# Wide attention: values held as weights, softmax sums from a block of ones, and a reordered load block

## The chip, the cores and the metric

The kernel runs on one core of a Trainium2 chip. The metric is the device time of one execution in microseconds (us). Before the change three executions took 2512.74 us in the median (2504.58 to 2514.27).

## What is computed

x is 16 sequences of 256 rows of 128 floats. Eight layers follow one another, each x = x + layer(layernorm(x)); the kernel has them in six blocks: wide attention, experts with slope attention, experts with rope attention, group attention, a recurrent layer, group attention. Only the first and the loads ahead of it are changed:

```python
def _L0_attn_a_ref(x, Wq, Wk, Wv, Wo, bo):          # N_HEADS = 16, HEAD_DIM = 64, DIM = 128
    q = (x @ Wq).reshape(b, s, N_HEADS, HEAD_DIM)    # likewise k and v
    dot = jnp.einsum('bihd,bkhd->bhik', q, k)
    w = jax.nn.softmax(dot / jnp.sqrt(jnp.float32(HEAD_DIM)), axis=-1)
    a = jnp.einsum('bhij,bjhd->bihd', w, v)
    return a.reshape(b, s, N_HEADS * HEAD_DIM) @ Wo + bo
...
x = x + _L0_attn_a_ref(_layernorm(x, axis=-1), L0_attn_a_Wq, L0_attn_a_Wk, L0_attn_a_Wv, L0_attn_a_Wo, L0_attn_a_bo)
```

## The kernel before, in words

x stays in SBUF for the whole kernel (`K.X`, 32 tiles of 128 rows, two a sequence). The program is a row of blocks; at the end of each all engines meet.

**Load block** (`load`, L95 to L185). SyncE's queue issues four transfers of x (L115) and then every weight of every layer in the order in which the program lists them (L117), the wide layer's five (`w_q`, `w_k`, `w_v`, `w_o`, `b_o`) last, then one small transfer `rows_dram` (L119), and waits for all (L120, L121). Meanwhile GpSimd (POOL) builds constants, and VectorE (DVE) takes the statistics of the 32 tiles once all of x is there (L184).

**Wide block** (`wide_attention`, L1905 to L2174). It begins with the layer norm's factors (`norm_stats`, L188, used by every layer), while POOL fills the ones' column of `va`, `parts` and the table `pick` (L2160 to L2168); the table takes a fill and six selects over 128x2048 elements. VectorE waits for those (L2134), scales `w_q` (L2136), and only then may TensorE start (L2036).

The work of sequence n + 1 (stage A), n (stage B) and n - 1 (stage E) is interleaved by `wide_schedule` (L1880) in nine slots; every engine walks the same list:
- A: `norm` turns the normalized rows (L1966), `qk` makes q and k of a pair of heads (L1972, copied by ScalarE at L2054, cast to bf16 by POOL at L2157), `max` makes bf16 scores (L1983) whose row maxima VectorE takes (L2098), `v` makes the values (L1976, copied by VectorE at L2089), `split` and `turnmax` bring the maxima into rows (L2101 to L2110).
- B: `score` makes the scores turned, keys on the partitions: two bf16 matmuls with `pick` put the negated maximum into the bank (L1999) and four f32 matmuls add k.q (L2003); ScalarE takes the exponential (L2059). `value` (L2014) multiplies: the probabilities are the stationary operand (128x128, four loads a head), and the values with a column of ones are the moving one (65 columns). So the sum stands beside the 64 outputs, queries on the partitions. `divide` is a reciprocal of 128x4 (L2116) and a product (L2118).
- E: `attn` turns the result by 16 transposes (L2023), copied by VectorE (L2093), and `project` multiplies by `w_o` (L2032), VectorE adds it to x (L2124) and takes the statistics (L2129).

Two PSUM banks hold the maxima (`Sb`), two the scores (`Tb`), two the values' output (`Ob`), and two are shared by all other pieces (`Mb`, with the semaphores `full` and `drained`). An f32 matmul and its weight load appear as two records each in the trace, an f32 transpose and a bf16 matmul as one. In `scores` and `maxima` the two heads of a pair lie on partitions 0 to 63 and 64 to 127 and use the two row halves of the array.

Elsewhere, in the group layer's `value` (L724), the values are already the stationary operand: four heads of 32 columns each write to four partition ranges of one bank.

## Time and profile before

| | |
|---|---|
| median of three executions | 2512.74 us |
| profiled execution, its own time | 2513.31 us |
| its span, first to last instruction | 2511.3 us |
| load block | 0 to 40.3 us |
| wide block | 40.3 to 788.3 us |
| busy in the whole span: TensorE, VectorE, ScalarE, POOL | 86%, 57%, 46%, 24% |

All durations below are from the profiled execution. PE is TensorE, PEld its weight loads, DVE VectorE, ACT ScalarE, POOL GpSimd, SPq the DMA issues of SyncE. In a timeline a row gives the start and the time up to the end of what it merges; the start of the next row of the same engine says when the array could go on, since the ends overlap the next piece.

### The profile page before, as it was taken

What the parts mean: (1) busy time and instruction counts of PE and PEld (TensorE: products, weight loads), DVE (VectorE), ACT (ScalarE), POOL (GpSimd) and SP (SyncE); (2) the same over time, 40 slices, a digit from 0 to 9 for tenths busy, and PEclk for the clock granted to TensorE, in tenths of its full rate; (3) what the DMA queues carried; (4) which work ended last, traced back from release to release, by engine and by line L of the source; (5) the groups of instructions that cost most, each with busy time, mean ns of one, the idle gap of its engine ahead of it and who ended that gap; (6) DMA issues with size and microseconds to landing.
All of it is one profiled execution on the core that took longest, in us unless ns stands there. A gap on an engine that the chain in (4) does not pass through costs nothing. (4 is left out here: it accounts for less than half of the span.)

```text
span 2511.3 us, 53791 instructions
## 1 busy us (share of the span) xinstructions
PE 2157.5 (86%) x21439; PEld 1560.5 (62%) x21439; DVE 1429.7 (57%) x2854; ACT 1158.7 (46%) x1979; POOL 602.0 (24%) x952
## 2 busy tenths in 40 slices
PE   0899999999998799788868998999669997469996
PEld 0687877877787689655547896666435543234543
DVE  1545454454542443466644445776568885768883
ACT  0333333333324233366553323665647775537774
POOL 4111111111100322133203232443123331433330
PEclk9999999999997899899978998999869998669998
DMA  5000000000000002245400022444134440034441
GB/s 156 1 1 1 1 1 1 1 1 1 1 1 1 6 5 51 51 108 117 95 2 4 1 52 53 109 116 93 25 84 107 110 105 2 2 92 108 107 106 49
DMA packets 142790, 121.04 MB, mean 48 GB/s; under 512 B 11808, under 2 KB 127408, under 8 KB 142548
## 3 DMA queue, kind: packets, MB, share of 16 engines
q1 hardware_dynamic: 142548, 117.64, 19.7%
q8 instruction: 172, 2.82, 0.5%
q14 instruction: 70, 0.57, 0.1%
HBM read 63.48 MB, written 54.12 MB: 47 GB/s over the span
## 5 line engine op out<-in xcount | busy, mean ns | idle before, releaser
L890 DVE TENSOR_REDUCE l_group_mx<-maxima 128x4 f32<-128x1024 f32 x248 | 303.9, 1226 | 77.1 <-PE maxima L683 75.6
L2059 ACT ACTIVATE l_wide_pr<-scores 128x512 f32<-128x512 f32 x256 | 139.0, 594 | 408.7 <-PE scores L2003 408.7
L818 ACT ACTIVATE l_group_pr<-scores 128x1024 f32<-128x1024 f32 x256 | 261.7, 1022 | 72.2 <-PE scores L704 70.0
L2014 PEld LDWEIGHTS bank<-l_wide_va,l_wide_pr 128*128 128x128 f32 x2048 | 254.2, 192 | 36.0 <-issue 33.2
L2014 PE MATMUL bank<-l_wide_va,l_wide_pr 128*128 128x65 f32 x2048 | 254.5, 271 | 0.0
L2098 DVE TENSOR_REDUCE l_wide_mx<-maxima 128x2 f32<-128x512 f32 x256 | 165.1, 687 | 92.2 <-PE maxima L1983 92.2
L2157 POOL CAST l_wide_qk<-l_wide_qk 128x512 bf16<-128x512 f32 x128 | 78.7, 615 | 390.6 <-ACT l_wide_qk L2054 390.6
L890 DVE TENSOR_REDUCE l_slope_mx<-maxima 128x6 f32<-128x768 f32 x124 | 118.9, 959 | 78.2 <-PE maxima L690 76.8
L890 DVE TENSOR_REDUCE l_rope_mx<-maxima 128x6 f32<-128x768 f32 x124 | 118.8, 958 | 58.8 <-PE maxima L690 57.9
L818 ACT ACTIVATE l_slope_pr<-scores 128x768 f32<-128x768 f32 x128 | 103.6, 810 | 91.0 <-PE scores L711 90.8
L724 PE MATMUL bank<-l_group_pr,va 128*32 128x256 f32 x2048 | 145.3, 403 | 0.0
L683 PE MATMUL maxima<-l_group_st 50*128 50x256 bf16 x992 | 102.4, 286 | 45.7 <-DMA l_group_st<-mask_dram 16.9
L818 ACT ACTIVATE l_rope_pr<-scores 128x768 f32<-128x768 f32 x128 | 103.8, 811 | 77.4 <-PE scores L711 77.2
L2003 PE MATMUL scores<-l_wide_qk 64*128 64x256 f32 x1024 | 132.3, 378 | 0.0
L2093 DVE COPY l_wide_att_t<-bank 128x512 f32<-128x512 f32 x64 | 44.3, 692 | 140.8 <-PE bank L2023 140.8
L704 PE MATMUL scores<-l_group_st 53*128 53x256 bf16 x1024 | 103.3, 281 | 16.4 <-ACT l_group_pr L818 11.8
L2054 ACT ACTIVATE l_wide_qk<-bank 128x512 f32<-128x512 f32 x128 | 76.4, 597 | 72.6 <-PE bank L1972 72.6
L2003 PEld LDWEIGHTS scores<-l_wide_qk 64*128 64x128 f32 x1024 | 99.2, 190 | 10.0
L683 PEld LDWEIGHTS maxima<-l_group_st 50*128 50x128 bf16 x992 | 35.2, 97 | 89.0 <-DVE l_group_mx L890 40.3
L1972 PE MATMUL bank<-l_wide_xnt,w_q 128*128 128x256 f32 x256 | 88.1, 426 | 0.5 <-ACT l_wide_xnt L2051 0.5
L1613 ACT ACTIVATE l_rope_e_ht<-maxima 128x512 f32<-128x512 f32 x64 | 38.1, 595 | 108.5 <-PE maxima L1562 108.4
L1613 ACT ACTIVATE l_slope_e_ht<-maxima 128x512 f32<-128x512 f32 x64 | 38.1, 595 | 107.3 <-PE maxima L1562 107.2
(456 smaller groups left out, 4721.5 us busy)
## 6 DMA issues: line engine op xcount, KB each, us to landing
l_group_st<-stack_dram SPq DMA_DIRECT2D x64, 384.0 KB, 6.0
l_slope_st<-stack_dram SPq DMA_DIRECT2D x32, 384.0 KB, 5.6
l_rope_st<-stack_dram SPq DMA_DIRECT2D x32, 384.0 KB, 5.6
stack_dram<-l_group_parts SPq DMA_DIRECT2D x64, 192.0 KB, 2.3
stack_dram<-l_group_parts SPq DMA_DIRECT2D x64, 128.0 KB, 1.9
stack_dram<-l_slope_parts SPq DMA_DIRECT2D x32, 192.0 KB, 2.4
stack_dram<-l_rope_parts SPq DMA_DIRECT2D x32, 192.0 KB, 2.3
stack_dram<-l_slope_parts SPq DMA_DIRECT2D x32, 128.0 KB, 2.3
```

What stands on the lines that cost most here:

```text
L683: ins = pe.matmul(Mx[:, z, first:first + keys], st[at, b % KEEP, 0, i, t * P:(t + 1) * P], st[at, b % KEEP, 1, i, 0:keys], start=(t == 0 o ...
L704: ins = pe.matmul(Tp[:, z, t * S:t * S + S - first], st[at, b % KEEP, 1, i, t * P:(t + 1) * P], st[at, b % KEEP, 0, i, first:S], start=(t ...
L724: ins = pe.matmul(Ob[i // 2][32 * z:32 * z + 32, (i % 2) * S + first:(i % 2) * S + S], va[:, b % KEEP, t, h // G, :], pr[:, (h // 2) % AHE ...
L818: act.activation(pr[:, i % AHEAD, :, 0:keys], Tp[:, :, 0:keys], ACT.Exp).then_inc(s["exps"], 1)
L890: dve.tensor_reduce(mx[:, b % 2, :, :, i], max_bank(i, b)[:, :, 0:BLOCKS * keys].rearrange("p z (a k) -> p z a k", k=keys), AX.X, ALU.max, ...
L1972: ins = pe.matmul(bank[:, z * S:(z + 1) * S], w[:, i * P:(i + 1) * P], xnt[:, nxt, :], start=True, stop=True)
L2003: ins = pe.matmul(Tb[z][:, t * S:(t + 1) * S], qk[rows(z), par, i, 1, t * P:(t + 1) * P], qk[rows(z), par, i, 0, :], start=False, stop=(t ...
L2014: ins = pe.matmul(Ob[i // 2 % 2][:, col:col + D64 + 1], pr[:, i % WIDE_AHEAD, kt * S + t * P:kt * S + (t + 1) * P], va[:, par, kt, i, :], ...
L2054: act.activation(qk[:, nxt, i].rearrange("p z s -> p (z s)"), Mb[b][:], ACT.Copy).then_inc(drained[b], 1)
L2059: act.activation(pr[:, h % WIDE_AHEAD, :], Tb[h % 2][:], ACT.Exp).then_inc(s["exps"], 1)
L2098: dve.tensor_reduce(mx[:, nxt, :, h], Sb[h % 2][:].rearrange("p (t k) -> p t k", k=S), AX.X, ALU.max, negate=True).then_inc(s["maxed"], 1)
L2157: pool.tensor_copy(qk16[:, nxt, i], qk[:, nxt, i]).then_inc(s["half"], 1)
```

## The change

Load block: SyncE issues x, then `w_q` and `w_k` (waited for in the block), then `w_v`, `w_o`, `b_o` (with a semaphore of their own, waited for in the wide block), then `rows_dram`. The 22 other transfers move to SyncE of the wide block. Each quarter of x has its own semaphore, and VectorE starts on a quarter when it has come. `pick` is made in this block: POOL builds a 128x16 table, and ScalarE spreads it to 128x16x128; `parts` and a 128x64 block of ones are filled here too.

Wide block: the list of pieces is one walk over all sequences (`wide_slots`, `wide_walk`), eight slots a sequence. In `value` the stationary operand is a head's 128x64 values and the moving one the probabilities (128x256); head z of a pair writes partitions 64z to 64z + 63. POOL adds the two key tiles of the probabilities (two additions of 128x256 a pair), and in `sum` a 128x64 block of ones as weights gives the sums, repeated on 64 partitions. `divide` becomes a reciprocal of 128x256 and a product of 128x256, which writes `att_t` directly: `attn`, its transposes and copies go. ScalarE copies the values instead of VectorE. `project` is split into two pieces.

```diff
-def load(nc, K, loads):
+def load(nc, K, first, behind, behind_s):
...
-                sp.dma_start(K.X[:, tiles, :], K.x_in[:, tiles, :]).then_inc(x_loaded, 16)
-            for dst, src in loads:
+                sp.dma_start(K.X[:, tiles, :], K.x_in[:, tiles, :]).then_inc(x_loaded[n], 16)
+            for dst, src in first:
                 sp.dma_start(dst, src).then_inc(loaded, 16)
+            for dst, src in behind:
+                sp.dma_start(dst, src).then_inc(behind_s, 16)
             sp.wait_ge(rows_copied, 1)
             sp.dma_start(K.rows_dram, row_rows[:]).then_inc(rows_kept, 16)
-            sp.wait_ge(loaded, 16 * len(loads))
+            sp.wait_ge(loaded, 16 * len(first))
...
+            act.wait_ge(eye_built, 1)
+            act.activation(K.pick[:], heads_eye[:].unsqueeze(2).to_broadcast([P, H, P]), ACT.Copy).then_inc(picked, 1)
...
+            c.done(pool.memset(heads_eye[:], 0.0))
+            for z in range(2):
+                for j in range(3):
+                    select(heads_eye[:], ALU.not_equal, 1.0, -(64 * z + H * j), [[-1, H]], 1)
+            pool.sem_inc(eye_built, 1)
+            c.done(pool.memset(K.ones[:], 1.0))
+            c.done(pool.memset(K.parts[:], 0.0))
...
+                if t % (TILES // parts) == 0:
+                    dve.wait_ge(x_loaded[t // (TILES // parts)], 16)
...
+def wide_slots():
+    slots = []
+    for i in range(PAIRS):
+        slot = [("divide", (i - 2) % PAIRS, -1 if i < 2 else 0), ("score", i, 0)]
+        slot += [("turnmax", 0, 1)] if i == 7 else []
+        slot += [("max", (i + 1) % PAIRS, 2 if i + 1 >= PAIRS else 1)]
+        slot += [("split", 0, 1)] if i == 6 else []
+        slot += [("qk", (i + 2) % PAIRS, 2 if i + 2 >= PAIRS else 1)]
+        slot += [(what, (i - 1) % PAIRS, -1 if i < 1 else 0) for what in ("value", "sum")]
+        slot += {1: [("v", 0, 1)], 2: [("v", 1, 1)], 3: [("v", 2, 1), ("xn", 0, 2)], 4: [("project", 0, -1)],
+                 5: [("v", 3, 1), ("norm", 0, 2)], 6: [("project", 1, -1)]}.get(i, [])
+        slots += slot
+    return slots
...
+        def max_banks(i, b):
+            return Tb if b == 0 and i % 2 else Sb
...
+        @block.sync
+        def _(sp):
+            for dst, src in late:
+                sp.dma_start(dst, src).then_inc(late_s, 16)
+            sp.wait_ge(behind_s, 16 * 3)
+            sp.wait_ge(late_s, 16 * len(late))
...
-                        if i % 2 == 0:
-                            wait(pe, s["divided"], o_t.add() - 2)
-                        pe.wait_ge(s["exps"], exps_t.add())
-                        for t in range(NT):
-                            col = ((i % 2) * NT + t) * (D64 + 1)
-                            for kt in range(NT):
-                                ins = pe.matmul(Ob[i // 2 % 2][:, col:col + D64 + 1],
-                                                pr[:, i % WIDE_AHEAD, kt * S + t * P:kt * S + (t + 1) * P], va[:, par, kt, i, :],
-                                                start=(kt == 0), stop=(kt == NT - 1))
-                        ins.then_inc(s["valued"], 1)
...
+                    wait(pe, s["divided"], p - 1)
+                    pe.wait_ge(s["exps"], 2 * p + 2)
+                    for kt in range(NT):
+                        for z in range(2):
+                            ins = pe.matmul(Ob[i % 2][rows(z), 0:S], va[:, at, kt, 2 * i + z, :],
+                                            pr[:, i % 2, z, kt * S:(kt + 1) * S], start=(kt == 0), stop=(kt == NT - 1))
+                    ins.then_inc(s["valued"], 1)
+                elif what == "sum":
+                    pe.wait_ge(s["added"], 2 * p + 2)
+                    for z in range(2):
+                        ins = pe.matmul(Ob[i % 2][rows(z), S:2 * S], ones[:], tiles_sum[:, i % 2, z, :], start=True, stop=True)
+                    ins.then_inc(s["summed"], 1)
+                elif what == "project":
+                    pe.wait_ge(s["divided"], PAIRS * (b + 1))
+                    for c in range(PAIRS):
+                        ins = pe.matmul(bank[:, 0:C], att_t[:, at, c, i * P:(i + 1) * P], W["wo"][:, c, :],
+                                        start=(c == 0), stop=(c == PAIRS - 1))
...
+                elif what == "v":
+                    act.wait_ge(full[m], count)
+                    act.activation(va[:, at, i // 2, 8 * (i % 2):8 * (i % 2) + 8, :].rearrange("p h d -> p (h d)"),
+                                   Mb[m][:], ACT.Copy).then_inc(drained[m], 1)
+                elif what == "score":
+                    wait(act, s["valued"], p - 1)
+                    wait(act, s["added"], 2 * (p - 1))
+                    for z in range(2):
+                        act.wait_ge(s["scored"], 2 * p + z + 1)
+                        act.activation(pr[:, i % 2, z, :], Tb[z][:], ACT.Exp).then_inc(s["exps"], 1)
...
-            dve.wait_ge(s["pool_set"], POOL_SETS)
...
+                elif what == "divide":
+                    dve.wait_ge(s["summed"], p + 1)
+                    wait(dve, s["divided"], p)
+                    own.done(dve.reciprocal(rc[:], Ob[i % 2][:, S:2 * S]))
+                    dve.tensor_tensor(att_t[:, at, i, :], Ob[i % 2][:, 0:S], rc[:], ALU.mult).then_inc(s["divided"], 1)
...
+                elif what == "score":
+                    wait(pool, s["summed"], p - 1)
+                    for z in range(2):
+                        pool.wait_ge(s["exps"], 2 * p + z + 1)
+                        pool.tensor_tensor(tiles_sum[:, i % 2, z, :], pr[:, i % 2, z, 0:S], pr[:, i % 2, z, S:2 * S],
+                                           ALU.add).then_inc(s["added"], 1)
...
+        late, first, behind = loads[:-5], loads[-5:-3], loads[-3:]
...
-                wide_attention(nc, K, name, W_wide)
+                wide_attention(nc, K, name, W_wide, late, behind_s, late_s)
```

In the new list POOL casts `qk` after the two additions of the slot, VectorE takes `divide` of the pair before last ahead of the slot's maxima, and TensorE's order in a slot is score, (turnmax), max, qk, value, sum, and then v, norm or half of project where the slot has one.

## Rows read from the trace of the kernel before

**Rows 1.** Windows, 400 to 500 us: PE, PEld, DVE, ACT, POOL busy; clock, DMA.

```profile
400.00:500.00 100.00, 98.39 (x751) 80.03 (x750) 49.90 (x107) 33.15 (x63) 13.75 (x22) 1.00 0.00 1
```

**Rows 2.** Timeline of PE: start, us, line, tiles, count, idle before.

```profile
402.10 0.61 PE L2023 MATMUL bank<-ident,l_wide_att 128*128 128x128 f32 x4
402.54 1.00 PE L2014 MATMUL bank<-l_wide_va,l_wide_pr 128*128 128x65 f32 x8
403.48 0.39 PE L1999 MATMUL scores<-l_wide_shift,l_wide_pick 64*128 64x512 bf16 x2
...
404.57 0.38 PE L1983 MATMUL maxima<-l_wide_qk 64*128 64x256 bf16 x4
404.88 0.70 PE L1972 MATMUL bank<-l_wide_xnt,w_q 128*128 128x256 f32 x2
...
405.85 1.00 PE L2014 MATMUL bank<-l_wide_va,l_wide_pr 128*128 128x65 f32 x8
...
426.75 3.84 PE L2032 MATMUL bank<-w_o,l_wide_att_t 128*128 128x128 f32 x32
...
434.15 0.39 PE L1999 MATMUL scores<-l_wide_shift,l_wide_pick 64*128 64x512 bf16 x2
...
436.58 0.39 PE L1999 MATMUL scores<-l_wide_shift,l_wide_pick 64*128 64x512 bf16 x2 [0.81 <-ACT l_wide_pr L2059]
...
745.86 0.39 PE L1999 MATMUL scores<-l_wide_shift,l_wide_pick 64*128 64x512 bf16 x2
...
773.40 3.68 PE L2014 MATMUL bank<-l_wide_va,l_wide_pr 128*128 128x65 f32 x32
```

**Rows 3.** Timeline of all engines, load block and start of the wide block.

```profile
10.51 6.29 DVE L184 BATCH_NORM_STATS2 moments<-x 128x6 f32<-128x128 f32 x32 [10.51 <-DMA x<-in_L_attn_a_x_dram]
...
33.31 0.53 SPq L119 DMA_DIRECT2D rows_dram<-row_rows  x1
...
42.84 12.77 POOL L2168 TENSOR_SCALAR_AFFINE_SELECT l_wide_pick<-l_wide_pick 128x2048 bf16<-128x2048 bf16 x6
...
56.91 0.69 PE L1966 MATMUL bank<-ident,l_wide_xn 128*128 128x128 f32 x2 [51.79 <-DVE w_q L2136]
```

**Rows 4.** Transfers, 0 to 100 us: GB/s in 40 slices of 2.5 us.

```profile
GB/s 32 282 290 292 229 108 61 356 406 326 289 287 150 390 346 55 3 3 0 0 0 0 0 0 0 0 0 0 0 0 0 0 7 0 0 0 0 0 0 0
```

**Rows 5.** Timeline of DVE, the same norm factors at the slope block's start.

```profile
788.37 0.21 DVE L196 TENSOR_TENSOR mean<-moments 128x32 f32<-128x32 f32 x1 [1.10 <-PEq L1908]
...
790.28 0.19 DVE L213 SCALAR_TENSOR_TENSOR shift<-mean,rstd 128x32 f32<-128x32 f32 x1
```

**Rows 6.** Timeline, first sequence's q, k and maxima, up to its first score.

```profile
68.60 0.60 ACT L2054 ACTIVATE l_wide_qk<-bank 128x512 f32<-128x512 f32 x1 [1.25 <-PE bank L1972]
...
69.37 0.62 POOL L2157 CAST l_wide_qk<-l_wide_qk 128x512 bf16<-128x512 f32 x1 [1.23 <-ACT l_wide_qk L2054]
...
77.04 0.39 PE L1983 MATMUL maxima<-l_wide_qk 64*128 64x256 bf16 x4 [0.40 <-DVE l_wide_mx L2098]
...
80.49 0.39 PE L1999 MATMUL scores<-l_wide_shift,l_wide_pick 64*128 64x512 bf16 x2 [0.39 <-DVE l_wide_shift L2110]
```

**Rows 7.** Timeline of PE, group layer: values as weights in four column ranges.

```profile
2033.01 1.07 PE L724 MATMUL bank<-l_group_pr,va 128*32 128x256 f32 x16
2034.02 0.39 PE L704 MATMUL scores<-l_group_st 53*128 53x256 bf16 x4
```

**Rows 8.** Groups by line and shape: busy us, mean ns, idle before.

```profile
L2116 DVE RECIPROCAL l_wide_rc<-bank 128x4 f32<-128x4 f32 x128 | 23.2, 181 | 69.7 <-PE bank L2014 63.2
L211 DVE RECIPROCAL rstd<-rstd 128x32 f32<-128x32 f32 x8 | 2.8, 353 | 2.6 <-ACT rstd L217 2.4
...
L2118 DVE TENSOR_TENSOR l_wide_att<-bank,l_wide_rc 128x256 f32<-128x256 f32 x128 | 54.3, 424 | 4.4
L2098 DVE TENSOR_REDUCE l_wide_mx<-maxima 128x2 f32<-128x512 f32 x256 | 165.1, 687 | 92.2 <-PE maxima L1983 92.2
L2153 POOL TENSOR_TENSOR x<-x,b_o 128x256 f32<-128x256 f32 x16 | 11.6, 725 | 190.4 <-ACT l_wide_xn L2066 190.4
```

More of the change, by code:

```diff
@@ L99, in load @@
         loaded = nc.alloc_semaphore(name="loaded")
-        x_loaded = nc.alloc_semaphore(name="x_loaded")
+        x_loaded = [nc.alloc_semaphore(name=f"x_loaded{n}") for n in range(4)]
         own = nc.alloc_semaphore(name="pool_own")
@@ L1874 @@
 D64 = 64
-WIDE_BANK = {"norm": (0,), "qk": (1, 0, 1, 0, 1, 0, 1, 0), "attn": (1, 0, 1, 0), "v": (1, 0, 1, 0), "project": (1,),
-             "turnmax": (0,)}
-WIDE_AHEAD = 4
-def wide_schedule(do_a, do_b, do_e):
-    early_a = {0: [("norm", 0)], 1: [("qk", 0), ("qk", 1)], 2: [("qk", 2), ("qk", 3)], 3: [("max", 0), ("qk", 4)],
-               4: [("max", 2), ("qk", 6)], 5: [("max", 4), ("v", 1)], 6: [("max", 6), ("v", 3)], 7: [("split", 0)],
-               8: [("turnmax", 0)]}
-    late_a = {3: [("max", 1), ("qk", 5)], 4: [("max", 3), ("qk", 7), ("v", 0)], 5: [("max", 5), ("v", 2)], 6: [("max", 7)]}
-    early_e = {1: [("attn", 0)], 2: [("attn", 2)], 7: [("project", 0)]}
-    late_e = {1: [("attn", 1)], 2: [("attn", 3)]}
-    pieces = []
-    for slot in range(PAIRS + 1):
-        if do_b and slot < PAIRS:
-            pieces.append(("score", slot))
-        for a, e, head in ((early_a, early_e, 0), (late_a, late_e, 1)):
-            if do_a:
-                pieces += a.get(slot, [])
-            if do_e:
-                pieces += e.get(slot, [])
-            if do_b and slot > 0:
-                pieces.append(("value", 2 * slot - 2 + head))
-        if do_b and slot > 0:
-            pieces.append(("divide", slot - 1))
-    return pieces
@@ L1905, in wide_attention @@
-def wide_attention(nc, K, name, W):
-    fills = [sum(b == m for banks in WIDE_BANK.values() for b in banks) for m in range(2)]
+def wide_slots():
[11 more added lines that the diff above has]
+    return slots
@@ new lines, in wide_walk @@
+def wide_walk():
+    slots, order, counts = wide_slots(), [], [0, 0]
+    bank = {}
+    for what, i, _ in slots:
+        if what in ("norm", "qk", "v", "project", "turnmax"):
+            bank[what, i] = len(bank) % 2
+    for n in range(-2, NB + 1):
+        for what, i, ahead in slots:
+            if 0 <= n + ahead < NB:
+                m = bank.get((what, i))
+                if m is not None:
+                    counts[m] += 1
+                order.append((what, i, n + ahead, m, counts[m] if m is not None else None))
+    return order
@@ L1933, in wide_attention @@
         block = ctx.enter_context(nc.Block(name))
-        POOL_SETS = 6
-        def rows(h):
-            return slice(64 * (h % 2), 64 * (h % 2) + 64)
-        def fill_tallies():
-            return [Tally(s["full0"], fills[0]), Tally(s["full1"], fills[1])]
-        def bank_of(tallies, what, i):
-            if what not in WIDE_BANK:
-                return None, None
-            b = WIDE_BANK[what][i]
-            return b, tallies[b].add()
+        order = wide_walk()
+        filling = {(what, i, b): (m, count) for what, i, b, m, count in order}
@@ L2140, in _ @@
+            dve.wait_ge(s["stats"], TILES)
         @block.gpsimd
         def _(pool):
[L2142 to L2157 removed]
@@ L2173, in _ @@
-            ins.then_inc(set_, 3)
-            batches(pool, tallies, step)
+            for what, i, b, m, count in order:
+                at, p = b % 2, PAIRS * b + i
+                if what == "norm":
+                    pool.wait_ge(s["xn"], b + 1)
+                    if b == 0:
+                        pool.wait_ge(behind_s, 16 * 3)
+                    x = K.X[:, b * NT:(b + 1) * NT, :]
+                    pool.tensor_tensor(x, x, W["bias"].unsqueeze(1).to_broadcast([P, NT, C]), ALU.add).then_inc(s["biased"], 1)
+                elif what == "qk":
+                    pool.wait_ge(drained[m], count)
+                    pool.sem_inc(s["waited"], 1)
+                    pool.tensor_copy(qk16[:, at, i], qk[:, at, i]).then_inc(s["half"], 1)
+                elif what == "score":
+                    wait(pool, s["summed"], p - 1)
+                    for z in range(2):
+                        pool.wait_ge(s["exps"], 2 * p + z + 1)
+                        pool.tensor_tensor(tiles_sum[:, i % 2, z, :], pr[:, i % 2, z, 0:S], pr[:, i % 2, z, S:2 * S],
+                                           ALU.add).then_inc(s["added"], 1)
@@ L2273, in program @@
         W_wide = {"wq": w_q[:], "wk": w_k[:], "wv": w_v[:], "wo": w_o, "bias": b_o[:]}
-        load(nc, K, loads)
+        K.ones, K.parts, K.pick = sb("ones", [P, D64]), sb("parts", [P, 2, NT, 2, 64], BF16), sb("pick", [P, H, P], BF16)
+        late, first, behind = loads[:-5], loads[-5:-3], loads[-3:]
+        for_wide.enter_context(nc.cleanup_on_exit())
+        behind_s, late_s = nc.alloc_semaphore(name="behind"), nc.alloc_semaphore(name="late")
+        load(nc, K, first, behind, behind_s)
         for n, layer in enumerate(LAYERS):
```

308 lines of the change are left out of this document (110 added, 198 removed).

## The prediction, made before the changed kernel had run

> **What bounds the kernel now.** I read the windows first. In the middle of the wide block TensorE is busy for 98.39 of 100 us at full clock, VectorE for 49.9, ScalarE for 33.2, POOL for 13.8 [rows 1]. So there the time is TensorE's list of pieces, and an edit on another engine counts only if TensorE waits for it. Next the timeline of PE, with the cost of a piece taken as the distance to the next start [rows 2]. The first score of one sequence starts at 434.15, that of the sequence seven later at 745.86: 44.53 us a sequence. A score piece costs 403.48 to 404.57 = 1.09, a max piece 0.31, a qk piece 0.97, a value piece of one head 402.54 to 403.48 = 0.94 (four in a row take 3.68, so 0.92; I use 0.93), a transpose piece 0.44, project up to 3.8 for both halves. At the start of each sequence TensorE waits 0.81 us for the exponentials of slot 0.
>
> The value pieces, 16 x 0.93 = 14.9 us, are a third of a sequence. A head is four f32 products of 65 columns. A qk piece streams two f32 products of 256 columns in 0.97 us, so by columns four of 65 would take about half of the 0.93: the weight loads of 128 columns set their pace.
>
> Last, the timeline of all engines up to TensorE's first real work [rows 3]. SyncE issues its last transfer at 33.31 us, the blocks change at 40.3, POOL then builds `pick` from 42.84 to 55.61, and TensorE starts at 56.91 with [51.79 <-DVE w_q]: VectorE's scaling of `w_q` stands behind POOL's table. Nothing but loading and preparation happens for 57 us.
>
> **The load block.** It ends when `rows_dram` has landed. After the change it stands behind x and the wide layer's five transfers only, 4160 KB instead of 9.8 MB (the slices together). The first four slices move 2.24 MB in 10 us [rows 4], and x is complete at 10.51 [rows 3]. The 2.1 MB left, at the 290 to 400 GB/s of the full slices, take 5.3 to 7.2 us, then `rows_dram` and the change of block about 1.5: 17 to 19, I take 18. Other work in this block is earlier: POOL's list grows by eight small operations and a fill, and ScalarE's spread of 2048 elements a partition, by 0.60 us for 512 [rows 6], is at most 2.4 us. Gain **22.3 us**. The 22 transfers that move to SyncE of the wide block have that queue to themselves, nobody there waits for them, and the wide block is far longer than their 30 us; POOL's queue issues none.
>
> **Start of the wide block.** The norm factors take 788.37 to 790.47 = 2.1 us where no POOL work runs beside [rows 5], and `w_q` 1.3 more (55.61 to 56.91 with the wait [rows 3]). So TensorE starts 3.5 us into the block, not 16.6: gain **13.1 us**.
>
> **First sequence.** Before, TensorE's start to its first score was 56.91 to 80.49 = 23.6 us [rows 3, 6], with four qk pieces made ahead. The new walk has max(i + 1) and then qk(i + 2), so each pair waits for its own chain: qk 0.97, to ScalarE 0.2, copy 0.60, to POOL 0.17 (68.60 + 0.60 to 69.37), cast 0.62, to TensorE 0.1, max 0.31 = 2.97 us [rows 2, 6]. Norm and the first qk and cast take about 4.5 us, seven steps 20.8, split and turnmax 3.5 less the wait already in 77.04 to 80.49 [rows 6], and qk of the next sequence stands before the score, 1.3: in all 29.8. Loss **6.2 us**. If TensorE stays at half clock (it did in its first pieces), up to 7 x 1.3 = 9 more.
>
> **A sequence in steady state.** Value and sum of a pair become six f32 products of 256 columns in two column halves. The wide trace has no 64-column weights. Nearest is the group layer: eight such products in four column ranges take 2033.01 to 2034.02 = 1.01 us [rows 7], where one after another at half a qk piece (0.43 to 0.49) they would take over 3.4. So ranges run side by side. With two ranges six products are three rounds of 0.43 = 1.28, plus the 0.15 that the 1.01 has over two rounds, plus 0.11 for a weight load that nothing covers: 1.55 us a pair, where 2 x 0.93 = 1.86 stood. Bounds: 1.3 if all loads hide, 2.85 if halves don't overlap. I take 1.55, since rows 7 is the same product with only the width changed. Sequence: 44.53 - 14.9 - 4 x 0.44 - 0.8 (score 0 now has max, qk, value and sum behind it) + 8 x 1.55 + 0.1 (project in two) = **39.5 us**.
>
> The Trainium skill, TensorEngine Tiling, Key Properties, says that a change of tiling mode drains the array, and the new slot goes row halves, full, column halves, row halves. If each of 128 value groups paid a drain of 0.17 us, what 402.10 + 0.61 overlaps its successor by, instead of my 0.11, the sum would be 8 us higher; no row here shows a change from full to column halves.
>
> **What covers the rest.** VectorE: copies of values and `att_t` leave it, and the reciprocal grows from 4 to 256 elements a partition. It takes 0.181 us for 4 and 0.353 for 32 [rows 8], so 6.1 ns an element and 1.72 us. A slot is 1.72 + 0.42 (product) + 2 x 0.69 (maxima) + 0.1 = 3.6 us against TensorE's 1.09 + 0.31 + 0.97 + 1.55 = 3.92; the slots with split or project are longer on TensorE too. Hidden, with 0.3 us to spare in the barest slot. The divide is needed only two slots later. POOL: two additions of at most 0.73 each (the row has a repeated operand, a lower bound; 1.0 is my upper) and a cast: 2.1 to 2.6 of 3.92. The cast ends near 4.1 after the slot's start, and its max starts at 3.92 + 1.09 = 5.0: hidden, 0.9 to spare. ScalarE adds four copies of 0.6 a sequence to a third of its time: hidden. If one of these covers goes, the stall is in TensorE's order before max or value.
>
> **Sum.** After the first score: first sequence (no value of a former one, no project) 39.5 - 1.55 - 3.8 = 34.2; 13 x 39.5 = 513.5; the last but one without look-ahead (0.31 + 2 x 0.97 + 0.45) 36.8; the last, eight scores and groups 8 x 2.64 + 3.8 = 24.9; the end 1.55 + 0.5 (additions) + 2.3 (divide) + 3.7 (project) + 1.0 + 1.1 = 10.2. Together 619.6, against 80.49 to 788.3 = 707.8: gain **88.2 us**. Total 22.3 + 13.1 - 6.2 + 88.2 = 117.4 us. The profiled execution took 2513.3, half a microsecond over the median: **2396 us**. Other blocks don't change.
>
> **Rivals.**
> - *Load and start alone.* The groups cost what they replace, 2.2 us with the transposes, because loads of weights expose themselves in column halves too. Then 2513.3 - 22.3 - 13.1 + 6.2 = 2484. For it: value is paced by loads today. Against: rows 7, where 16 loads hide in 1.01 us. Chance 0.07.
> - *VectorE becomes the bound.* If the reciprocal from PSUM takes 3.0 rather than 1.72 us, a sequence on VectorE is 8 x (3.0 + 0.42 + 1.37 + 0.2) + 2.4 = 42.3 and TensorE waits for maxima: 2.8 x 15.5 = 43 more, 2440. It decides from 2.6 us on. For it: 256 elements are eight times the longest reciprocal seen. Against: the slope from 4 to 32. Chance 0.09.
> - *Slower.* The column halves don't run side by side: value and sum stream 6 x 0.43 and cost 2.85 a pair. 128 pairs x 1.3 = +166: 2562. It decides from 0.92 us a pair on, where the 117.4 are gone, that is at 2.47. For it: no 64-column weights in the trace, and `sum` adds a third to the columns. Against: rows 7. Chance 0.05.
>
> **Numbers.** The forecast has 0.79. Its range: 1.3 instead of 1.55 a pair is -32, so 2364, with little chance; a further 0.15 a pair for switches +19, a first sequence at half clock +9, uneven slots with short VectorE stalls of 1 us a sequence +15: 2439, which also reaches the second rival. Range 2368 to 2442. A difference under 0.5%, 12.6 us, can't be told from none: faster 0.94 (the first two rivals too), same 0.01, slower 0.05.
>
> **What would show it.** Start of wide block near 18 and first PE piece 3.5 later; a new L for value and sum with starts 1.5 to 1.6 us apart; first scores of consecutive sequences 39.5 apart; reciprocal near 1.72 us; PE over 97% busy there with no wait on VectorE. A reciprocal over 2.6 us or groups over 2.4 would make me wrong; so would PE idling before max behind POOL's cast.

## The result, and the profile after

The changed kernel took 2400.79 us in the median of four executions (2398.14 to 2402.08), the kernel before beside it 2509.22. The ratio is 0.9566, 95% interval [0.9542, 0.9590]: faster. The profiled execution took 2402.08 us with a span of 2400.2. Forecast were 2396 us and 2368 to 2442.

The windows of the steady state (us, then PE, PEld, DVE, ACT, POOL busy, clock, DMA) answer to [rows 1]:

```profile
400.00:500.00 100.00, 100.00 (x717) 61.72 (x717) 77.04 (x106) 41.51 (x77) 40.82 (x63) 1.00 0.00 1
```

TensorE has no gap left, its weight loads are busy for 62 instead of 80 of 100 us, and VectorE rose from 50 to 77. The timeline of PE over a bare slot, one with a piece v and one with half of project answers to [rows 2] and [rows 7]:

```profile
308.26 1.13 PE L1997 MATMUL bank<-w_v,l_wide_xnt 128*128 128x512 f32 x2
309.32 0.39 PE L2020 MATMUL scores<-l_wide_shift,pick 64*128 64x512 bf16 x2
...
313.23 2.05 PE L2046 MATMUL bank<-w_o,l_wide_att_t 128*128 128x128 f32 x16
315.21 0.39 PE L2020 MATMUL scores<-l_wide_shift,pick 64*128 64x512 bf16 x2
...
330.53 0.39 PE L2020 MATMUL scores<-l_wide_shift,pick 64*128 64x512 bf16 x2
330.75 1.03 PE L2024 MATMUL scores<-l_wide_qk 64*128 64x256 f32 x8
331.62 0.38 PE L2004 MATMUL maxima<-l_wide_qk 64*128 64x256 bf16 x4
331.93 0.70 PE L1991 MATMUL bank<-l_wide_xnt,w_q 128*128 128x256 f32 x2
...
332.99 1.08 PE L2035 MATMUL bank<-l_wide_pr,l_wide_va 128*64 128x256 f32 x8
333.90 0.60 PE L2041 MATMUL bank<-l_wide_tiles_sum,ones 128*64 128x256 f32 x4
334.44 0.39 PE L2020 MATMUL scores<-l_wide_shift,pick 64*128 64x512 bf16 x2
...
370.54 0.39 PE L2020 MATMUL scores<-l_wide_shift,pick 64*128 64x512 bf16 x2
```

Value costs 332.99 to 333.90 = 0.91 us and sum 0.54, together 1.45 a pair (forecast 1.55). The bare slot is 330.53 to 334.44 = 3.91 (forecast 3.92), but qk takes 1.06 where it took 0.97, v 1.06 and half of project 1.98. The next sequence starts at 370.54: 40.01 us a sequence, forecast 39.5, before 44.53.

The load block and start, timeline of all engines, answer to [rows 3, 5, 6]:

```profile
5.02 1.64 DVE L200 BATCH_NORM_STATS2 moments<-x 128x6 f32<-128x128 f32 x8 [5.02 <-DMA x<-in_L_attn_a_x_dram]
...
9.10 2.08 SPq L123 DMA_DIRECT2D rows_dram<-row_rows  x1
...
16.04 0.24 POOL L147 TENSOR_SCALAR_AFFINE_SELECT not_first<-not_first 64x80 bf16<-64x80 bf16 x1
...
17.41 0.21 DVE L212 TENSOR_TENSOR mean<-moments 128x32 f32<-128x32 f32 x1 [5.36 <-PEq L97]
...
20.56 0.66 PE L1985 MATMUL bank<-ident,l_wide_xn 128*128 128x128 f32 x2 [15.45 <-ACT l_wide_xn L2059]
...
25.23 0.61 PE L2004 MATMUL maxima<-l_wide_qk 64*128 64x256 bf16 x4 [1.47 <-POOL l_wide_qk L2129]
...
29.31 0.61 PE L2004 MATMUL scores<-l_wide_qk 64*128 64x256 bf16 x4 [1.47 <-POOL l_wide_qk L2129]
...
41.14 0.39 PE L2004 MATMUL maxima<-l_wide_qk 64*128 64x256 bf16 x4 [0.61 <-POOL l_wide_qk L2129]
...
44.06 0.39 PE L2004 MATMUL scores<-l_wide_qk 64*128 64x256 bf16 x4 [0.61 <-POOL l_wide_qk L2129]
```

The wide block starts at 17.4 (forecast 18) and TensorE 3.2 us later (3.5). Then the first sequence: its maxima wait for POOL's cast as forecast, at first 4.08 us apart (25.23 to 29.31), later 2.92 (41.14 to 44.06; forecast 2.97). The early ones run their pieces at half the pace (the w_q part of a qk piece takes 25.77 to 26.78 = 1.01 us, later 41.46 to 42.00 = 0.54), and this lasts to about 38 us. The clock column of the windows reads 1.00 there, so it doesn't show this; the pieces do. The first score comes at 54.67.

Groups by line and shape, for [rows 8]:

```profile
L2105 DVE RECIPROCAL l_wide_rc<-bank 128x256 f32<-128x256 f32 x128 | 224.4, 1753 | 56.7 <-PE bank L2041 55.7
L2106 DVE TENSOR_TENSOR l_wide_att_t<-bank,l_wide_rc 128x256 f32<-128x256 f32 x128 | 54.3, 425 | 4.4
L2134 POOL TENSOR_TENSOR l_wide_tiles_sum<-l_wide_pr 128x256 f32<-128x256 f32 x256 | 180.5, 726 | 359.5 <-ACT l_wide_pr L2077 359.5
```

The reciprocal takes 1.753 us (forecast 1.72), the addition 0.726 (at most 0.73 to 1.0).

**Where the 111 us of the two profiled spans are.** The block behind the wide one starts at 788.37 before and at 687.11 after: 101.3 us come from load and wide block. The rest of the span is 1722.9 before and 1713.1 after, though nothing in it was changed. Stretches of all runs of this study, read from the timelines:

| run | wide block starts | first PE | first score | a sequence | wide block ends | rest of the span | median, us |
|---|---|---|---|---|---|---|---|
| before | 40.3 | 56.9 | 80.5 | 44.53 | 788.4 | 1722.9 | 2505 to 2513 |
| after | 17.4 | 20.6 | 54.7 | 40.01 | 687.1 | 1713.1 | 2400.8 |
| after_again | 18.1 | 21.3 | 54.7 | 40.01 | 686.1 | 1713.3 | 2404.1 |
| load_only | 18.0 | 21.1 | 44.5 | 44.53 | 752.7 | 1718.9 | 2472.2 |
| loads_first | 40.5 | 43.6 | 79.4 | 40.01 | 710.7 | 1706.9 | 2421.1 |
| one_half | 17.4 | 20.6 | 54.7 | 50.32 | 845.2 | 1723.1 | 2565.8 |
| short_reciprocal | 17.4 | 20.5 | 53.9 | 40.01 | 681.9 | 1722.4 | 2403.1 |
| product_twice | 18.0 | 21.1 | 55.0 | 40.01 | 688.1 | 1724.4 | 2409.1 |
| no_sum | 17.4 | 20.6 | 54.1 | 36.56 | 634.8 | 1713.3 | 2351.5 |
| bf16_sums | 17.3 | 20.5 | 54.5 | 37.43 | 646.6 | 1712.1 | 2371.0 |
| together | 18.1 | 21.2 | 54.7 | 38.98 | 670.4 | 1716.1 | 2393.0 |
| early_qk | 17.4 | 20.5 | 43.9 | 40.01 | 673.6 | 1722.4 | 2397.8 |
| both | 18.0 | 21.2 | 44.0 | 38.98 | 656.6 | 1709.6 | 2372.4 |
| all_three | 17.4 | 20.5 | 43.4 | 36.40 | 616.5 | 1718.1 | 2337.9 |

A sequence repeats to 0.01 us. The load block ends at 17.3 to 18.1 with the same code, and the wide block of the changed kernel at 687.1 and 686.1: its last piece, project, took 6.53 us at a granted clock of 0.56 in the one execution and 5.44 at 0.69 in the other. The rest of the span scatters by 17 us, and this goes with the clock too: the four runs where the windows show 0.91 for it (loads_first, both, bf16_sums, no_sum) took 1706.9 to 1713.3 us, the ten at 0.90 took 1713.1 to 1724.4. What lowers the clock wasn't tested. So effects are read from the stretches up to the end of the wide block, 1 to 3 us being open at that end, and the medians say whether they arrive.

### The profile page after: what moved, and what is told of

Its sections match the earlier page's. It is cut to its first block and busy times, and to the rows that moved or that the text cites. A ratio compares the mean times of both kernels' runs of the same rounds, so it can differ in the third digit from the quotient of the medians.

```text
span 2400.2 us, 52498 instructions
## 1 busy us (share of the span) xinstructions
PE 2097.6 (87%) x20671; PEld 1388.0 (58%) x20671; DVE 1555.6 (65%) x2742; ACT 1197.1 (50%) x2044; POOL 762.4 (32%) x1208
## 3 DMA queue, kind: packets, MB, share of 16 engines
q1 hardware_dynamic: 142548, 117.64, 20.6%
## 5 line engine op out<-in xcount | busy, mean ns | idle before, releaser
L906 DVE TENSOR_REDUCE l_group_mx<-maxima 128x4 f32<-128x1024 f32 x248 | 304.0, 1226 | 72.3 <-PE maxima L699 70.6
L2134 POOL TENSOR_TENSOR l_wide_tiles_sum<-l_wide_pr 128x256 f32<-128x256 f32 x256 | 180.5, 726 | 359.5 <-ACT l_wide_pr L2077 359.5
L2105 DVE RECIPROCAL l_wide_rc<-bank 128x256 f32<-128x256 f32 x128 | 224.4, 1753 | 56.7 <-PE bank L2041 55.7
L2089 DVE TENSOR_REDUCE l_wide_mx<-maxima 128x2 f32<-128x512 f32 x248 | 159.4, 685 | 32.5 <-PE maxima L2004 32.5
L2035 PE MATMUL bank<-l_wide_pr,l_wide_va 128*64 128x256 f32 x1024 | 138.8, 392 | 0.3 <-DVE l_wide_att_t L2106 0.3
L1001 POOL CAST l_group_cols<-l_group_mx 128x32 bf16<-128x32 f32 x32 | 6.7, 209 | 317.1 <-DVE l_group_mx L906 317.1
L2035 PEld LDWEIGHTS bank<-l_wide_pr,l_wide_va 128*64 128x64 f32 x1024 | 62.1, 136 | 61.0 <-issue 36.1
L2070 ACT ACTIVATE l_wide_va<-bank 128x512 f32<-128x512 f32 x64 | 38.2, 597 | 116.1 <-PE bank L1997 116.1
```

The source lines that it names most:

```text
L906: dve.tensor_reduce(mx[:, b % 2, :, :, i], max_bank(i, b)[:, :, 0:BLOCKS * keys].rearrange("p z (a k) -> p z a k", k=keys), AX.X, ALU.max, ...
L2035: ins = pe.matmul(Ob[i % 2][rows(z), 0:S], va[:, at, kt, 2 * i + z, :], pr[:, i % 2, z, kt * S:(kt + 1) * S], start=(kt == 0), stop=(kt == ...
L2089: dve.tensor_reduce(mx[:, at, :, 2 * i + z], max_banks(i, b)[z][:].rearrange("p (t k) -> p t k", k=S), AX.X, ALU.max, negate=True).then_in ...
L2105: own.done(dve.reciprocal(rc[:], Ob[i % 2][:, S:2 * S]))
L2134: pool.tensor_tensor(tiles_sum[:, i % 2, z, :], pr[:, i % 2, z, 0:S], pr[:, i % 2, z, S:2 * S], ALU.add).then_inc(s["added"], 1)
```

## The experiments

`load_only` is made from the kernel before, all others from the changed one.

**after_again**, the changed kernel itself. 

> The changed kernel once more, beside the kernel before on the same chip. Its wide block ended at 687 us against 788.3, a gain of 101 us, and everything behind it took 1713 against 1723 us though nothing there was changed. Theory (the 10 us behind the wide block are scatter between executions): the ratio is 0.957 to 0.960, and the blocks behind the wide one come within a few us of 1715 to 1723 again without a fixed sign. Rival (the change makes the later blocks faster, by its layout in SBUF or its loads): they take 1713 again and the kernel before 1723.

Measured: 2404.09 us, ratio 0.9599 [0.9581, 0.9618]. The rest took 1713.3 us again, which alone would fit the rival, but over all runs of the changed code it went from 1706.9 to 1724.4, both sides of the kernel before. The kernel before was profiled only once, but its medians of 2505.6 to 2509.2 lie 4 to 8 us under that profiled execution, so its 1722.9 is a long one. The 10 us are scatter; the change is worth what the end of the wide block shows, 101 to 102 us.

**load_only**, the old attention behind the new load block:

```diff
-        load(nc, K, loads)
+        load(nc, K, first, behind, behind_s)
...
+            for dst, src in late:
+                sp.dma_start(dst, src).then_inc(late_s, 16)
...
-        pick = sb("pick", [P, H, P], BF16)
+        parts, pick = K.parts, K.pick
```

> The kernel before with the new load block, pick and parts built there and the 22 late transfers in the wide block, and its old attention. Theory (load and start are worth 22.9 + 13.4 = 36 us and add to the rest): about 36 us under the kernel before, ratio 0.986, TensorE's first piece near 21 us, a sequence 44.5 us as before. Rival (the early start is lost again at once, because late transfers disturb the first sequence or the clock is lower): under 25 us.

Measured: 2472.18 us, ratio 0.9871 [0.9837, 0.9905], end of the wide block 788.4 to 752.7 = 35.7 us. The theory holds: the first score comes 36.0 us earlier, and nearly all of it is left at the end, so nothing is lost to the late transfers. It shows one thing more: TensorE's start to the first score takes 21.1 to 44.5 = 23.3 us with the old list and 20.6 to 54.7 = 34.1 with the new one. The new list costs 10.8 us here, not 6.2.

**loads_first**, the changed kernel with all transfers, and the waits for them, in the load block:

```diff
+            for dst, src in K.late:
+                sp.dma_start(dst, src).then_inc(K.late_s, 16)
             for dst, src in first:
                 sp.dma_start(dst, src).then_inc(loaded, 16)
...
+            sp.wait_ge(behind_s, 16 * 3)
+            sp.wait_ge(K.late_s, 16 * len(K.late))
```

> The changed kernel with all transfers in the load block again, in the old order. Theory (what ends the load block is the transfer issued last, and 5.6 MB of late weights stand ahead of it): the wide block starts near 40 instead of 17.4, the time is 23 us over the changed kernel, and TensorE starts 3.2 us into the block as in the changed kernel, since pick is not built there. Rival (POOL's longer list, which ended at 16.3, sets the block's end): under 5 us over it.

Measured: 2421.13 us, ratio 0.9670 [0.9649, 0.9692]; the wide block starts at 40.5, 23.1 us later, TensorE 3.2 us behind it, and the wide block ends 23.6 us later than after. The median is only 17 us over after_again; the rest of the span is the shortest of all here. Order of loads: 23 us of the 101.

**one_half**, no two column halves at once from the third pair on, the second head in columns of its own in the bank:

```diff
-                    for kt in range(NT):
-                        for z in range(2):
+                    for kt, z in [(kt, z) for kt in range(NT) for z in range(2)] if p < 2 else [(kt, z) for z in range(2) for kt in range(NT)]:
-                            ins = pe.matmul(Ob[i % 2][rows(z), 0:S], va[:, at, kt, 2 * i + z, :],
+                            ins = pe.matmul(Ob[i % 2][rows(z), 0:S] if p < 2 else Ob[i % 2][rows(0), z * S:(z + 1) * S],
+                                            va[:, at, kt, 2 * i + z, :],
...
-                        ins = pe.matmul(Ob[i % 2][rows(z), S:2 * S], ones[:],
+                        ins = pe.matmul(Ob[i % 2][rows(z), S:2 * S] if p < 2 else Ob[i % 2][rows(0), z * S:(z + 1) * S], ones[:],
```

> From the third pair on both heads' value and sum products write partitions 0 to 63, a head after the other, so that two column halves can't run at once; the sums and half of the outputs are then wrong values, the instructions are the same. Theory (the halves run side by side, value 0.91 us and sum 0.54): alone they stream 6 x 0.43 = 2.6 us, the slot grows by 1.2 us, 126 pairs, +140 to +160 us, which makes it slower than the kernel before by about 40. Rival (the group is limited by weight loads, not by columns): under +40 us.

Measured: 2565.77 us, ratio 1.0223 [1.0189, 1.0258], 50.32 us a sequence. Its timeline of PE:

```profile
331.82 1.94 PE L2034 MATMUL bank<-l_wide_pr,l_wide_va 128*64 128x256 f32 x8
333.60 1.03 PE L2040 MATMUL bank<-l_wide_tiles_sum,ones 128*64 128x256 f32 x4
334.56 1.12 PE L1997 MATMUL bank<-w_v,l_wide_xnt 128*128 128x512 f32 x2
```

The wide block ends 158 us later, inside the expected 140 to 160. The same products cost 1.78 and 0.96 instead of 0.91 and 0.54. The third rival's mechanism is real and has this price, +1.29 us a pair; the changed kernel is faster only because the halves do run side by side.

**short_reciprocal**, the divide's reciprocal over a quarter of the columns:

```diff
-                    own.done(dve.reciprocal(rc[:], Ob[i % 2][:, S:2 * S]))
-                    dve.tensor_tensor(att_t[:, at, i, :], Ob[i % 2][:, 0:S], rc[:], ALU.mult).then_inc(s["divided"], 1)
+                    own.done(dve.reciprocal(rc[:, 0:64], Ob[i % 2][:, S:S + 64]))
+                    dve.tensor_tensor(att_t[:, at, i, :].rearrange("p (a e) -> p a e", e=64), Ob[i % 2][:, 0:S].rearrange("p (a e) -> p a e", e=64),
+                                      rc[:, 0:64].unsqueeze(1).to_broadcast([P, 4, 64]), ALU.mult).then_inc(s["divided"], 1)
```

> The changed kernel with the reciprocal taken of 64 of the 256 queries and used four times over (wrong sums for three quarters), so that it costs some 0.55 us instead of 1.75. Theory (VectorE is hidden behind TensorE in every slot of the steady state): a sequence stays at 40.0 us, and only the end and the last sequence gain, 2 to 5 us in all. Rival (VectorE holds TensorE back somewhere): a sequence falls under 39 us, 15 us or more in all.

Measured: 2403.14 us, ratio 0.9571 [0.9526, 0.9616]; 40.01 us a sequence, unchanged to the hundredth, and the wide block ends 5.2 us earlier, 5.0 of it behind the last sequence's start, where project runs at full pace (3.81 us) too. VectorE isn't on the path in the steady state.

**product_twice**, VectorE loaded with a second product a pair:

```diff
+                    own.done(dve.tensor_tensor(att_t[:, at, i, :], Ob[i % 2][:, 0:S], rc[:], ALU.mult))
                     dve.tensor_tensor(att_t[:, at, i, :], Ob[i % 2][:, 0:S], rc[:], ALU.mult).then_inc(s["divided"], 1)
```

> The changed kernel with the product of the divide done twice, 0.47 us more on VectorE a pair, so 4.1 us in a bare slot against TensorE's 3.91. Theory (bare slots have 0.3 us to spare, and the work may slip into the slots with v and project since the divide is needed only two slots later): under 1 us a sequence, 0 to 15 us in all. Rival (VectorE is close to the bound and every addition shows): 0.47 x 128 = 60 us.

Measured: 2409.12 us, ratio 0.9596 [0.9551, 0.9641], against 2400.8 and 2404.1. Windows:

```profile
400.00:500.00 100.00, 100.00 (x716) 61.61 (x716) 83.09 (x127) 41.25 (x77) 41.17 (x63) 1.00 0.01 1
```

VectorE is busy for 83 instead of 77 us of 100, and a sequence takes 40.01 us still; the wide block ends 1 to 2 us later. But the run doesn't push VectorE over TensorE's slot, as was expected of it (4.1 against 3.91). With no gap before it, a bare slot on VectorE takes 355.94 to 359.25 = 3.31 us in the changed kernel and 611.35 to 615.12 = 3.77 here:

```profile
355.94 1.74 DVE L2105 RECIPROCAL l_wide_rc<-bank 128x256 f32<-128x256 f32 x1
...
359.25 1.76 DVE L2105 RECIPROCAL l_wide_rc<-bank 128x256 f32<-128x256 f32 x1
```

```profile
611.35 1.74 DVE L2105 RECIPROCAL l_wide_rc<-bank 128x256 f32<-128x256 f32 x1
...
613.93 1.28 DVE L2089 TENSOR_REDUCE l_wide_mx<-maxima 128x2 f32<-128x512 f32 x2
615.12 1.75 DVE L2105 RECIPROCAL l_wide_rc<-bank 128x256 f32<-128x256 f32 x1
```

Operations that follow one another overlap a little (the maxima begin at 613.93 and take 1.28, the next reciprocal begins at 615.12), so that the prediction's 3.6 us, a sum of durations, was too long; the cover is 0.6 us a bare slot instead of 0.3. Whether longer slots would slip into those with v and project was not tested.

**no_sum**, the sum products left out from the third pair on:

```diff
+                    if p < 2:
+                        pe.wait_ge(s["added"], 2 * p + 2)
+                        for z in range(2):
+                            pe.matmul(Ob[i % 2][rows(z), S:2 * S], ones[:], tiles_sum[:, i % 2, z, :], start=True, stop=True)
...
-                elif what == "sum":
-                    pe.wait_ge(s["added"], 2 * p + 2)
-                    for z in range(2):
-                        ins = pe.matmul(Ob[i % 2][rows(z), S:2 * S], ones[:], tiles_sum[:, i % 2, z, :], start=True, stop=True)
-                    ins.then_inc(s["summed"], 1)
...
-                    dve.wait_ge(s["summed"], p + 1)
+                    dve.wait_ge(s["valued"], p + 1)
...
-                    wait(pool, s["summed"], p - 1)
+                    wait(pool, s["valued"], p - 1)
```

> The changed kernel without the sum products from the third pair on (the divide takes stale sums of the first pairs, so the output is wrong). Theory (TensorE's list is the bound and a sum piece costs 0.54 us): 126 x 0.54 = 68 us less if VectorE follows; its slot of 3.6 us is then longer than TensorE's 3.4, so 50 to 66 us less. Rival (VectorE or the chain over POOL sets the pace already): under 20 us less.

Measured: 2351.45 us, ratio 0.9372 [0.9322, 0.9421]; the wide block ends 52.3 us earlier, 3.45 us a sequence. The size is in the expected band, the reason given for the loss isn't: TensorE is busy for 100 of 100 us here too, and VectorE for 82, so VectorE doesn't bind; its bare slot of 3.31 us is still under TensorE's 3.47. A sum piece is worth 0.43 us, what two f32 products of 256 columns side by side take. The other 0.1 is the change of shape behind it, which then stands behind value: value to v takes 1.01 instead of 0.91 in this timeline of PE.

```profile
332.18 1.08 PE L2039 MATMUL bank<-l_wide_pr,l_wide_va 128*64 128x256 f32 x8
333.19 1.13 PE L1997 MATMUL bank<-w_v,l_wide_xnt 128*128 128x512 f32 x2
```

**bf16_sums**, where POOL rounds the added probabilities to bf16 and the block of ones is bf16:

```diff
-        tiles_sum = sb("tiles_sum", [P, 2, 2, S])
+        tiles_sum = sb("tiles_sum", [P, 2, 2, S], BF16)
...
-        K.ones, K.parts, K.pick = sb("ones", [P, D64]), sb("parts", [P, 2, NT, 2, 64], BF16), sb("pick", [P, H, P], BF16)
+        K.ones, K.parts, K.pick = sb("ones", [P, D64], BF16), sb("parts", [P, 2, NT, 2, 64], BF16), sb("pick", [P, H, P], BF16)
```

> The changed kernel with POOL writing the added probabilities as bf16 and the block of ones in bf16: the sum piece then streams 256 columns once instead of four times, 0.11 us for both halves, and costs about 0.2 instead of 0.54. Theory (TensorE's list is the bound): 128 x 0.3 = 38 us less, some of it lost where VectorE's 3.6 us slot then binds: 25 to 38 us. Rival (a switch between f32 and bf16 inside the column halves costs what the columns save): under 10 us.

Measured: 2370.96 us, ratio 0.9453 [0.9407, 0.9498]; 37.43 us a sequence, 0.32 a pair, and the wide block ends 40.5 us earlier (the median is 30 to 33 us lower). Nothing is lost to VectorE, as had been expected in part. The sum piece takes 0.20 us:

```profile
333.56 0.28 PE L2041 MATMUL bank<-l_wide_tiles_sum,ones 128*64 128x256 bf16 x2
333.76 2.05 PE L2046 MATMUL bank<-w_o,l_wide_att_t 128*128 128x128 f32 x16
```

**together**, pieces of the whole array next to each other:

```diff
-        slot += [(what, (i - 1) % PAIRS, -1 if i < 1 else 0) for what in ("value", "sum")]
         slot += {1: [("v", 0, 1)], 2: [("v", 1, 1)], 3: [("v", 2, 1), ("xn", 0, 2)], 4: [("project", 0, -1)],
-                 5: [("v", 3, 1), ("norm", 0, 2)], 6: [("project", 1, -1)]}.get(i, [])
+                 5: [("v", 3, 1)], 6: [("project", 1, -1)]}.get(i, [])
+        slot += [(what, (i - 1) % PAIRS, -1 if i < 1 else 0) for what in ("value", "sum")]
+        slot += [("norm", 0, 2)] if i == 5 else []
```

> The changed kernel with v and the halves of project moved from behind sum to right behind qk, so that pieces that use the whole array stand together and the slot changes shape once less. Theory (a change of shape costs an uncovered weight load or a drain, seen as v 1.06 and project 1.98 us behind sum where they took 0.97 and under 1.9 before): 0.1 us for each of six pieces, 0.5 to 0.7 us a sequence, 8 to 11 us in all. Rival (the cost only moves to the next piece, since value then meets the same change): within 3 us of the changed kernel.

Measured: 2392.99 us, ratio 0.9532 [0.9514, 0.9551]; 38.98 us a sequence, 1.03 less. Its timeline of PE:

```profile
304.35 0.70 PE L1992 MATMUL bank<-l_wide_xnt,w_q 128*128 128x256 f32 x2
...
305.31 1.95 PE L2047 MATMUL bank<-w_o,l_wide_att_t 128*128 128x128 f32 x16
307.19 1.08 PE L2036 MATMUL bank<-l_wide_pr,l_wide_va 128*64 128x256 f32 x8
308.11 0.60 PE L2042 MATMUL bank<-l_wide_tiles_sum,ones 128*64 128x256 f32 x4
308.64 0.39 PE L2021 MATMUL scores<-l_wide_shift,pick 64*128 64x512 bf16 x2
```

qk in front of project takes 0.96 instead of 1.06, and project 1.88 instead of 1.98. The v pieces show the price by their neighbours. In the kernel before, v takes 547.19 to 548.05 = 0.86 us between two pieces of the whole array, and 550.38 to 551.35 = 0.97 behind a max piece, which uses row halves:

```profile
547.19 1.02 PE L1976 MATMUL bank<-w_v,l_wide_xnt 128*128 128x512 f32 x2
548.05 1.00 PE L2014 MATMUL bank<-l_wide_va,l_wide_pr 128*128 128x65 f32 x8
...
550.38 1.12 PE L1976 MATMUL bank<-w_v,l_wide_xnt 128*128 128x512 f32 x2
551.35 1.00 PE L2014 MATMUL bank<-l_wide_va,l_wide_pr 128*128 128x65 f32 x8
```

In the changed kernel it stands between column halves (sum) and row halves (score) and takes 1.06; in together it has qk ahead and column halves behind, 0.96:

```profile
329.98 1.02 PE L1998 MATMUL bank<-w_v,l_wide_xnt 128*128 128x512 f32 x2
330.94 1.08 PE L2036 MATMUL bank<-l_wide_pr,l_wide_va 128*64 128x256 f32 x8
```

So v, qk and project, which use the whole array, pay 0.1 us for a neighbour in halves on either side, and it makes no difference here whether these are row or column halves. A score piece too takes 1.18 instead of 1.09 where a piece of the whole array follows (559.16 to 560.34 in the kernel before). The new place saves two of these in each of five slots (4.97 to 4.77, 5.89 to 5.70 us); the slot that has norm too gains only 0.05, since norm stays behind sum. Together that is the 1.03. It is more than was expected because I had counted one a piece.

**early_qk**, a list of its own for the first sequence:

```diff
+    first = "xn0 norm0 qk0 qk1 qk2 max0 qk3 max1 qk4 v0 xn8 max2 qk5 max3 qk6 v1 max4 qk7 max5 v2 max6 v3 max7 norm8 split0 qk8 turnmax0 max8 qk9"
...
-    for n in range(-2, NB + 1):
+    for n in range(0, NB + 1):
```

> The changed kernel with a list of its own for the first sequence: three qk pieces ahead of the first max, v between. Theory (the first score, at 54.7 us, is late because each pair waits for its own chain from TensorE over ScalarE and POOL, at half clock for the first half): TensorE is busier, the clock rises earlier, the first score comes 9 to 12 us earlier and the time falls as much. Rival (VectorE's maxima, 1.4 us a pair, or the clock hold it): under 5 us.

Measured: 2397.75 us, ratio 0.9548 [0.9533, 0.9563]. The first score comes at 43.9 instead of 54.7, 10.8 us earlier. The wide block ends 13.5 us earlier, but the other 2.7 lie at its other end: project ran at full pace here, 3.81 us at a granted clock of 1.00 instead of 6.53 at 0.56, behind the same wait of 3.2. Of the gain the median shows 3 to 6 us, with a rest of 1722.4 us in the profiled run. In the windows TensorE is busy for 22.25 of the 25 us, 18.34 in the changed kernel, and its pieces reach full pace at 27 us instead of 38. The windows, and the project piece at the end:

```profile
20.00:45.00 25.00, 22.25 (x100) 12.41 (x100) 12.78 (x24) 10.69 (x20) 7.22 (x12) 1.00 0.74 212
```

```profile
667.54 3.81 PE L2055 MATMUL bank<-w_o,l_wide_att_t 128*128 128x128 f32 x32 [3.22 <-DVE l_wide_att_t L2115]
```

**both**, together and early_qk with

```diff
-                    pe.wait_ge(s["divided"], PAIRS * (b + 1))
                     for c in range(PAIRS):
+                        if i == 0:
+                            pe.wait_ge(s["divided"], PAIRS * b + c + 1)
```

> together and early_qk at once, and project waits for each pair's divide by itself instead of for all eight, which matters only at the end of the block. Theory (different stretches, so they add): 8 to 11 and 9 to 12, and 1 to 3 at the end: 18 to 26 us under the changed kernel. Rival (with TensorE's slots shorter, VectorE binds and part is lost): under 15.

Measured: 2372.44 us, ratio 0.9466 [0.9439, 0.9492]; the wide block ends at 656.6, 30.5 us earlier, more than the 18 to 26 expected. Its parts: 10.6 up to the first score, 0.4 and 1.3 in the first and the last but one sequence, 1.04 x 13 = 13.5 between them, and 4.6 in the last sequence and the end. Of these 4.6, early_qk had 2.7 by the pace of project alone; the 1.9 left come with the single waits, where TensorE works on project while the last divides run. No run has these waits alone.

**all_three**, both and bf16_sums:

> both, with the bf16 sums. bf16_sums alone was 33 us under the changed kernel by medians. Theory: the gains add, 50 to 58 us under the changed kernel, near 2350. Rival (the bare slots are then bound by VectorE's 3.6 us and what together saves is lost there): the gain over bf16_sums is under 15 us.

Measured: 2337.86 us, ratio 0.9318 [0.9301, 0.9335], 33 us under bf16_sums. The wide block ends 70.6 us earlier than after. The gain is larger than the expected 50 to 58: TensorE is still at 100 of 100 us and VectorE at 81 in the windows, so the rival's bound isn't reached. Whoever accepts sums rounded to bf16 gets this kernel; without the rounding `both` is the best one here.

## Why the prediction was right, and where

- **The bound.** That TensorE's list sets the pace is shown from both sides: a shorter list is faster (no_sum, bf16_sums, together), less or more work on VectorE changes nothing in a sequence (short_reciprocal, product_twice).
- **Load and start**, forecast 22.3 + 13.1: measured 22.9 + 13.4, alone in load_only 35.7. The order of loads is 23 of it (loads_first). What ends the block is `rows_dram` (landed by 17 us). POOL's last operation ends at 16.3, so only about 1 us more could be had here from the transfers alone.
- **Value and sum**, forecast 1.55 us a pair: measured 1.45. The side-by-side columns of four ranges carried over to two, and one_half shows what hung on it.
- **VectorE as cover**: right, and the cover is twice what was claimed, 0.6 us a bare slot. **POOL as cover**: right in the steady state, where TensorE has no gap, but no run loaded POOL by itself. In the first two slots of the block TensorE does wait for POOL's cast, 0.28 and 0.30 us.
- **First sequence**, forecast loss 6.2: it was 10.5 (34.1 against 23.6). The mis-sized term is the step of 2.97 us, 4.08 while pieces ran at half pace. The prediction named this as up to 9 us more and kept it out of the sum.
- **A sequence**, forecast 39.5: 40.01. (The prediction's own terms add up to 39.57.) What the sum left at the old prices is what changed: the eight qk pieces take 8.48 us instead of 7.54, the four v 4.13 instead of 3.75, project 3.97 instead of 3.67 and the 0.1 allowed, all by neighbours in halves. Against that, value and sum take 0.8 less than forecast, and three score pieces fewer have a piece of the whole array behind them, 0.1 each. Net 0.4 to 0.5 us a sequence, x 13, is 6 to 7 us.
- **First, last but one and last sequence and the end**, forecast 34.2, 36.8 and 35.1: 35.8, 37.7 and 38.8. The 1.6 hold 0.75 of waits (for POOL's cast and once for an exponential, 0.17), the 0.9 hold 0.24 of a wait for VectorE's shift; what is left wasn't taken apart, and the same changes of shape are in it. In the end, project waited 3.21 us for both last divides and then ran at half pace: 678.35, 6.53 us for what takes 3.96. That is 2.6 us of the 3.7, and it varies from run to run (5.44 in after_again, 3.81 in early_qk).
- Together 117.4 - 101.3 = 16 us too much gain. The median came within 5 us of the forecast because the unchanged blocks, counted at 1723 us, were executed in 1713: that part was luck. With 1723 the time would have been about 2411, still in the range.

TensorEngine Tiling (Array Packing) of the Trainium skill (Key Properties) says that a change of tiling mode drains the array. The runs show a price at such changes, 0.1 us on each side of a piece of the whole array, but not whether it is a drain or a weight load that nothing covers. The prediction had weighed the rule as 8 us, on the value groups. These came out cheaper than forecast; the cost stood at qk, v and project, and that the net of 6 to 7 us is near 8 is chance.

## What to carry to other kernels

Where TensorE is busy all the time and a group of matmuls takes longer than its columns account for (0.93 us for four products of 65 columns, about twice their share), make the short operand the stationary one and put two of them side by side in column ranges. That weight loads set the old pace was argued from this ratio; no run isolated it. The price is more elements on the engine that divides, and it is free only as long as that engine has slack. Then put pieces of one shape next to each other. Size a list's first and last passes by themselves, because a list that is tight in the steady state can be a plain chain in them.
